# Graph convolution and mixture of experts: chunk maxima spread by TensorE, gate weights second in their queue, x in batches, gathers of edges first in theirs

## What is computed

```python
edge_index = jnp.stack([src, dst])
h = _layernorm(x)                                   # m, v over the 512 columns
agg = jax.ops.segment_sum(h[src], dst, num_segments=2500)
x = x + (jax.nn.relu((h + agg) @ gW1 + gb1) @ gW2 + gb2)

t = _layernorm(x)
gate = jax.nn.softmax(t @ Wg, axis=-1)              # [2500, 8]
topv, topi = jax.lax.top_k(gate, 2)
topv = topv / (jnp.sum(topv, axis=-1, keepdims=True) + 1e-06)
scores = jnp.zeros((2500, 8)).at[jnp.arange(2500)[:, None], topi].set(topv)
for e in range(8):
    ye = jax.nn.gelu(t @ eW1[e] + eb1[e], approximate=False) @ eW2[e] + eb2[e]
    x = x + ye * scores[:, e:e + 1]
```

## Time and profile before

| | |
|---|---|
| median of 3 runs | 671.99 us (671.09 to 674.37) |
| profiled execution: its own time | 672.53 us |
| profiled execution: its span | 670.8 us |
| TensorE busy | 564.6 us, 84% |
| VectorE | 408.1 us, 61% |
| ScalarE | 298.4 us, 44% |
| GpSimd | 251.4 us, 37% |
| first stage: TensorE's first product of the first layer, first of the sums | 29.80 us, 142.46 us |

### The profile page before, as it was taken

One profiled execution on the slowest core, in us unless ns is written; L12 is line 12 of the kernel. 1 busy time (PEld: TensorE's weight loads), 2 busy tenths in 40 slices (PEclk: granted clock), 3 DMA queues, 4 the chain that ended last, 5 costly groups with the idle time before them and its releaser, 6 DMA issues.

```text
span 670.8 us, 10239 instructions
## 1 busy us (share of the span) xinstructions
PE 564.6 (84%) x3667; PEld 438.6 (65%) x3668; DVE 408.1 (61%) x776; ACT 298.4 (44%) x569; POOL 251.4 (37%) x215
## 2 busy tenths in 40 slices
PE   0597979999999999999999999904999999999800
PEld 0486868766756666766666655804888888889800
DVE  3562566777468877976986131696656675454441
ACT  0265346533233224223322300528676776767662
POOL 5044112213007004200700411013577878787763
PEclk9999889999899999999999999956999999999955
DMA  9351400020001220311121121878589988899994
GB/s 241 89 139 47 140 1 1 1 74 1 1 11 53 78 63 2 93 47 48 47 79 60 48 80 59 267 259 246 129 171 193 185 194 181 180 204 199 179 172 63
DMA packets 41672, 72.50 MB, mean 108 GB/s; under 512 B 11315, under 2 KB 15547, under 8 KB 41106
## 3 DMA queue, kind: packets, MB, share of 16 engines
q0 software_dynamic: 12864, 29.74, 22.9%
q1 hardware_dynamic: 27394, 37.44, 18.7%
q10 hardware_dynamic: 1364, 4.66, 2.5%
HBM read 46.70 MB, written 26.17 MB: 109 GB/s over the span
## 4 chain that ended last, share of the span: by engine, by line
PE 58%; DMA 13%; POOL 9%; ACT 6%; issue 6%; DVE 5%; SPq 1%; ACTq 1%; POOLq 0%; DVEq 0%
PE psum L1291 25%; PE psum L1275 9%; PE psum L1211 8%; DMA out_x<-y,target_i 8%; PE psum L1328 6%; POOL out_x L581 6%; POOL xg L574 3%; DMA Wg_sb<-in_L_ffn_Wg 3%; PE psum L1433 2%; PE psum L1422 2%; PE psum L1200 1%; ACT y L781 1%; DMA slot_rows<-edge_pairs,start_i 1%; DMA w_raw<-in_L_ffn_W 1%; ACT h L658 1%
## 5 line engine op out<-in xcount | busy, mean ns | idle before, releaser
L962 DVE TENSOR_TENSOR hot_key<-iota_key,key_w 128x1200 f16<-128x1200 f16 x125 | 113.6, 909 | 67.8 <-PE psum L1275 66.5
L640 ACT ACTIVATE counts<-psum 128x400 bf16<-128x400 f32 x125 | 61.8, 506 | 155.9 <-PE psum L1275 155.6
L1291 PE MATMUL psum<-counts,z_hi 125*128 125x500 bf16 x400 | 102.2, 376 | 2.2 <-ACT h L658 1.6
L581 POOL DMA_INDIRECT out_x<-y,target_i x54 | 90.5, 1676 | 35.8 <-issue 12.5
L1291 PE MATMUL psum<-counts,z_lo 125*128 125x500 bf16 x400 | 101.2, 376 | 0.0
L1275 PE MATMUL psum<-hot_key,hot_lo 128*128 128x200 f16 x750 | 82.6, 250 | 7.3 <-ACT counts L640 7.3
L548 POOL TENSOR_TENSOR h_lo<-h,h_hi 128x500 fp32r<-128x500 f32 x16 | 23.5, 1500 | 169.5 <-ACT h_hi L665 169.5
L1275 PEld LDWEIGHTS psum<-hot_key,hot_lo 128*128 128x128 f16 x750 | 66.1, 98 | 28.5 <-ACT counts L640 8.4
L962 DVE TENSOR_TENSOR hot_lo<-iota_lo,lo_w 128x768 f16<-128x768 f16 x125 | 83.6, 669 | 0.0
L1211 PE MATMUL psum<-W_sb,xT 128*125 128x256 f32 (+1 forms) x320 | 77.3, 397 | 0.0
L574 POOL DMA_INDIRECT xg<-xt_d,token_i x56 | 58.0, 1036 | 38.8 <-DVE token_i L1118 22.1
(11 more groups left out here) (226 smaller groups left out, 1056.3 us busy)
## 6 DMA issues: line engine op xcount, KB each, us to landing
w_raw<-in_L_ffn_W SPq DMA_DIRECT2D x16, 512.0 KB, 6.8
b_now<-in_L_ffn_b SPq DMA_DIRECT2D x27, 256.0 KB, 4.6
x_res<-in_x SPq DMA_DIRECT2D x20, 224.0 KB
out_x<-x SPq DMA_DIRECT2D x20, 224.0 KB
xt_d<-xt SPq DMA_DIRECT2D x20, 224.0 KB
x_in<-in_x ACTq DMA_DIRECT2D x2, 1120.0 KB
x_in<-in_x SPq DMA_DIRECT2D x2, 1120.0 KB
W_sb<-in_L_gnn_W ACTq DMA_DIRECT2D x1, 1024.0 KB, 7.6
```

The source lines that it names most:

```text
L581: pool.indirect_dma_start(out=out[:, :], in_=y[:, k % 2, i], in_offset=None, out_offset=bass.IndirectOffsetOnAxis(ap=target_i[:, 2 * k + i ...
L640: act.activation(counts[:, it % 2, :, place:place + W], psum[:, WIN + w % 2, 0:MW].rearrange("p (w h) -> p h w", w=W), ACT.Copy).then_inc( ...
L962: ins = dve.tensor_tensor(hot[:, w % RING].rearrange("p s (n two) -> p s n two", two=2), iota[:].rearrange("p (o n two) -> p o n two", o=1 ...
L1291: ins = mm(psum[:, AGG + c, 0:GN], half[:, t, c * 128:(c + 1) * 128], counts[0:P, g % 2, t], start=(t == 0 and n == 0), stop=(t == T - 1 a ...
```

## The change

- TensorE spreads the chunk maxima: VectorE multiplies an identity matrix with the maxima (`hit[:, 1]`, 125 x 625), and TensorE multiplies that with ones, which puts all 625 maxima on each partition, in PSUM (`spans_spread`). `find_chunks` reads them there. The way through memory (`spans_d`, `spans_b`) stays for the general case alone. TensorE may not write these banks at tile 1 before `chunks_known`.
- SP's queue: gate weights between dst and src; edge pairs ahead of `dst_next`.
- x is loaded in the five batches of the statistics, each with its own semaphore (`load_rows`): three at the start, by ScalarE's queue, the fourth and fifth by SP at the old places.
- GpSimd makes `ones`, the identity and what the first steps need first, tables for the general case last, and issues both gathers ahead of all `low_parts`.
- VectorE: new order, below. TensorE: W1 turned ahead of the gate sum.
- Flaws and first row transposes after tile 5 (was 7), the flag after tile 7 (was 9), so windows start after tile 8. The last statistics follow `one_hots(9)` (was 5), their scales `one_hots(11)`.

```diff
-ROWS_AT, FLAG_AT, ROWS_FIRST = 7, 9, 4
+ROWS_AT, FLAG_AT, ROWS_FIRST = 5, 7, 4
...
-        def load_half(eng, n):
+        def load_rows(eng, b):
+            a, end = BATCHES[b]
+            place = a % (2 * HALF)
             for cut in CUTS:
-                eng.dma_start(x_in[cut, HALF * (n % 2):HALF * (n % 2 + 1)], x_tiles[cut, HALF * n:HALF * (n + 1)]).then_inc(x_in_sems[n], 16)
+                eng.dma_start(x_in[cut, place:place + end - a], x_tiles[cut, a:end]).then_inc(x_in_sems[b], 16)
...
                 sp.dma_start(dst_i[cut], dst.rearrange("(p e) -> p e", p=P)[cut]).then_inc(S["dst_in"], 16)
+            sp.dma_start(Wg_sb[:], Wg.rearrange("(k p) e -> p k e", p=128)).then_inc(S["wg_in"], 16)
             for cut in CUTS:
                 sp.dma_start(src_i[cut], src.rearrange("(p e) -> p e", p=P)[cut]).then_inc(S["src_in"], 16)
-            sp.dma_start(Wg_sb[:], Wg.rearrange("(k p) e -> p k e", p=128)).then_inc(S["wg_in"], 16)
-            sp.wait_ge(S["spans_ready"], 1)
-            sp.dma_start(spans_d.rearrange("a (p c) -> p a c", p=P), spans[:]).then_inc(S["spans_out"], 16)
             sp.wait_ge(S["tables"], 1)
             sp.dma_start(edge_pairs[E:E + SLOTS, :].rearrange("(o e) a -> o e a", o=1), pad_pairs[:]).then_inc(S["rows_out"], 16)
-            sp.wait_ge(S["spans_out"], 16)
-            sp.dma_start(spans_b[:], spans_d.rearrange("(o a) c -> o a c", o=1).broadcast_to([NW, 2, NCH])).then_inc(S["spans_in"], 16)
+            sp.wait_ge(S["keys_ready"], 1)
+            for cut in CUTS:
+                sp.dma_start(edge_pairs[0:E, :].rearrange("(p e) a -> p (e a)", p=P)[cut],
+                             pairs_sb[cut].rearrange("p e a -> p (e a)")).then_inc(S["rows_out"], 16)
             sp.wait_ge(S["next_blank"], 1)
...
-            sp.wait_ge(S["keys_ready"], 1)
-            for cut in CUTS:
-                sp.dma_start(edge_pairs[0:E, :].rearrange("(p e) a -> p (e a)", p=P)[cut],
-                             pairs_sb[cut].rearrange("p e a -> p (e a)")).then_inc(S["rows_out"], 16)
...
-            load_half(sp, 2)
+            load_rows(sp, 3)
...
+            pool.memset(ones[:], 1.0)
+            step(pool.memset(ident[:], 0.0))
+            pool.affine_select(out=ident[:], in_=ident[:], compare_op=ALU.not_equal, fill=1.0, base=0,
+                               pattern=[[-1, 128]], channel_multiplier=1).then_inc(S["ident_ready"], 1)
+            pool.memset(eps_t[:], EPS)
+            pool.iota(win_lo[:], pattern=[[HW, 2]], base=0, channel_multiplier=W, **small)
+            pool.memset(pad_pairs[:, :, 0], PAST)
+            pool.memset(pad_pairs[:, :, 1], -1.0).then_inc(S["tables"], 1)
...
-            def low_parts(a, b):
-
-                for t in range(a, b):
-                    pool.wait_ge(S["z_ready"], t + 1)
-                    pool.wait_ge(S["z_hi_ready"], t + 1)
-                    pool.tensor_tensor(z_lo[:, t], z[:, t % ZF], z_hi[:, t], ALU.subtract).then_inc(S["z_lo_ready"], 1)
-
-            low_parts(0, 2)
+                               pattern=[[1, W], [-1, T]], channel_multiplier=0).then_inc(S["tables"], 1)
             pool.wait_ge(S["chunks_known"], 1)
             for a in range(2):
                 pool.indirect_dma_start(out=bound_rows[:, a], out_offset=None, in_=dst.rearrange("(c e) -> c e", e=CH),
                                         in_offset=bass.IndirectOffsetOnAxis(ap=chunk_i[:, a:a + 1], axis=0),
                                         bounds_check=NCH - 1).then_inc(S["bounds_gathered"], 16)
-            low_parts(2, 4)
+            pool.iota(win_hi[:], pattern=[[HW, 2]], base=HW - 1, channel_multiplier=W, **small)
+            pool.iota(chunk_up[:], pattern=[[1, NCH]], base=1, channel_multiplier=0, **small)
+            pool.iota(chunk_down[:], pattern=[[-1, NCH]], base=NCH, channel_multiplier=0, **small)
+            pool.iota(gen_iota[:], pattern=[[1, MW]], base=0, channel_multiplier=0, **small).then_inc(S["tables"], 1)
             pool.wait_ge(S["starts_known"], 1)
             pool.wait_ge(S["rows_out"], 48)
             for a in range(2):
                 pool.indirect_dma_start(out=slot_rows[:, a].rearrange("w e a -> w (e a)"), out_offset=None, in_=edge_pairs[:, :],
                                         in_offset=bass.IndirectOffsetOnAxis(ap=start_i[:, a:a + 1], axis=0)).then_inc(S["gathered"], 16)
-            low_parts(4, T)
+
+            def low_parts(a, b):
+
+                for t in range(a, b):
+                    pool.wait_ge(S["z_ready"], t + 1)
+                    pool.wait_ge(S["z_hi_ready"], t + 1)
+                    pool.tensor_tensor(z_lo[:, t], z[:, t % ZF], z_hi[:, t], ALU.subtract).then_inc(S["z_lo_ready"], 1)
+
+            low_parts(0, T)
...
-            for n in range(2):
-                load_half(act, n)
-            act.wait_ge(S["tables"], 2)
+            for b in range(3):
+                load_rows(act, b)
+            act.wait_ge(S["tables"], 1)
...
-            dve.tensor_reduce(spans[:, 1], dst_v, AX.X, ALU.max).then_inc(S["spans_ready"], 1)
+            step(dve.tensor_reduce(spans[:, 1], dst_v, AX.X, ALU.max))
+            dve.wait_ge(S["ident_ready"], 1)
+            dve.tensor_tensor(hit[:, 1].rearrange("p (c q) -> p c q", c=CPP), ident[0:P, 0:P].rearrange("p (o q) -> p o q", o=1).broadcast_to([P, CPP, P]),
+                              spans[:, 1].rearrange("p (c o) -> p c o", o=1).broadcast_to([P, CPP, P]), ALU.mult).then_inc(S["spans_wide"], 1)
...
-                dve.wait_ge(S["spans_in"], 16)
+                dve.wait_ge(S["spans_spread"], 1)
+                largest = psum[0:NW, AGG + 2:AGG + 4].rearrange("p b n -> p (b n)")[:, 0:NCH]
                 for a in range(2):
-                    step(dve.tensor_scalar(hit[:, a], spans_b[:, 1], win_lo[:, a:a + 1], None, ALU.is_lt, ALU.add,
+                    step(dve.tensor_scalar(hit[:, 0], largest, win_lo[:, a:a + 1], None, ALU.is_lt, ALU.add,
                                            accum_out=first[:, a:a + 1]))
...
-            edge_sources()
+            find_chunks()
+            weight_scale()
             centre_gate()
-            weight_scale()
             statistics(0)
             scales(0)
             scale_weights()
+            edge_sources()
+            edge_keys()
             statistics(1)
             scales(1)
-            edge_keys()
+            find_starts()
             statistics(2)
             scales(2)
-            find_chunks()
             compare_edges()
+            close_rows()
             statistics(3)
-            scales(3)
-            find_starts()
-            close_rows()
...
+            scales(3)
...
-                if w == 5:
+                if w == 9:
                     statistics(4)
+                if w == 11:
                     scales(4)
...
-            pe.wait_ge(S["tables"], 2)
+            pe.wait_ge(S["spans_wide"], 1)
+            for b in range(2):
+                part = slice(512 * b, min(512 * (b + 1), NCH))
+                ins = mm(psum[0:NW, AGG + 2 + b, 0:part.stop - part.start], ones[0:P].broadcast_to([P, NW]), hit[:, 1, part], start=True, stop=True)
+            ins.then_inc(S["spans_spread"], 1)
+            pe.wait_ge(S["ident_ready"], 1)
+            pe.wait_ge(S["w1_most_ready"], 1)
+            for m in range(KC):
+                ins = pe.transpose(psum[:, WIN, m * 128:(m + 1) * 128], W1_most[:, m * 128:(m + 1) * 128], ident[:])
+            ins.then_inc(S["w1_turned"], 1)
             pe.wait_ge(S["wg_in"], 16)
             for k in range(KC):
                 ins = mm(psum[:, WIN + 1, 0:NE], ones[:].broadcast_to([128, 128]), Wg_sb[:, k], start=(k == 0), stop=(k == KC - 1))
             ins.then_inc(S["wg_summed"], 1)
-            pe.wait_ge(S["w1_most_ready"], 1)
-            for m in range(KC):
-                ins = pe.transpose(psum[:, WIN, m * 128:(m + 1) * 128], W1_most[:, m * 128:(m + 1) * 128], ident[:])
-            ins.then_inc(S["w1_turned"], 1)
...
+                if t == 1:
+                    pe.wait_ge(S["chunks_known"], 1)
```

52 lines of the change are left out of this document (22 added, 30 removed).

## The result

The changed kernel takes 662.16 us (median of 4 runs, 661.56 to 664.91); the kernel before took 671.54 us beside it. The ratio is 0.986, interval 0.982 to 0.990. On a second chip it was 0.982 (0.976 to 0.988). Both intervals lie wholly under 1. So 9.4 us went, where 19.25 were forecast, and the time lies above the range of 647 to 660. The profiled execution took 661.56 us, its span 659.8.

The account below looks back on a forecast made before the run. TensorE was taken to bound the first stage: a late start on the gate weights, then a chain of 20 tiles with waits. - 8.0 + 2.2 - 7.35 - 6.0 + 2.0 - 2.1 = - 19.25 us, so 652.5 us; range 647 to 660.

Parts of the forecast that it names:

- Step 1, the start: Before the first layer: VectorE's new order and earlier gate weights start it at about 21.8 instead of 29.80; minus 8.0 us.
- the start does not come sooner: Rival: gate weights land at 20.8 as ever, small pieces slow beside x; minus 1.6, not 8.0; 659 us; chance 0.10.
- Step 2, tiles 0 to 5: First tiles: VectorE's edge steps ahead of statistics make TensorE late by 1.3 and 0.9; plus 2.2 us (0 to 4).
- Step 3, the rows: Flaws and row transposes after tile 5: wait for gathered rows goes, minus 4.35; full clock behind it, minus 3.0 us.
- The clock was to stay: At the row transposes and their tile: full clock instead of half, 5.2 us instead of 8.25; minus 3.0 us.
- Step 4, windows: From tile 8, two windows a tile: minus 2.1, minus 6.0 for the 4.47 wait and slow return, plus 2.0 us.
- The three waits fewer: Three windows come after the last tile alone, so three waits of 0.70 us for ScalarE go; minus 2.1 us.
- The new wait: At tile 13's transposes TensorE waits while ScalarE stands at the root for batch 4's statistics; plus 2.0 us (1 to 3.5).
- The clock rival: New short waits at tiles 1, 2 and 12 lower the clock, 1.5 to 3.0 us each; 655.5 to 659; chance 0.14.
- more waits than I see: Rival: the new order of three engines has further waits, such as late bound gathers; 660 to 668 us; chance 0.07.
- Faster: The whole kernel takes measurably less time than before, 0.5% (3.4 us) being distinguishable; chance 0.96.

Follow-up runs that it names:

- before_wg_behind_w1: The kernel before with one edit, the gate weights behind W1 in ScalarE's queue: 668.37 us, ratio 0.991.
- The three repairs: Changed kernel with gate weights behind W1, fourth statistics behind the flag, last statistics behind window 7: 651.81 us, ratio 0.964 to the kernel before.

## Why the prediction was wrong

**Step 1, the start: the failed step.** Minus 8.0 was forecast, minus 3.28 came. VectorE's steps had the right sizes: search 12.82 to 14.92 as in the sum, from PSUM at 0.86 and 0.87 a pass, no dearer than from SBUF; product 0.81, the lower bound (16.6 + 4.96 is 21.6 and not 21.8, a slip of 0.2). What failed is the sentence that bounded the gate weights' landing by 15.08, "the time at which the transfer in this place (src) landed". A place in a queue is not a time. Src has 125 pieces of 2.5 KB; the gate weights have 512, and from 8 to 16 us each waits for one of ScalarE's. They landed at 19.4. Of the 3.28, 1.36 is their landing (19.44 for 20.80) and 1.92 is W1's transposes and the weight scale, which are done while they are awaited. The rival "the start does not come sooner" named the cause, small pieces beside x, and was given 0.10; it would have been right to ask how many pieces there are, a number that stood in the prediction. The Trainium skill (DMA: Bandwidth & Descriptors, "Queues, rings and completion order") speaks of a packet of several pieces at a time, by which the prediction had the gate weights in by 9 to 13, an estimate. Page and trace differ, and the measurement decides: here the packets that the trace counts alternate one for one, in stretches as short as 0.2 us, each of the small ones a single piece of 32 bytes. Cost: 4.7 us, shown by two edits. The step also gave the 8.0 to VectorE's new order; before_wg_behind_w1 starts as early with the old one, so it was the gate weights' landing that held the start in the kernel before.

**Step 2, tiles 0 to 5.** Plus 2.2 forecast. From the first layer's start to the flaws' sum it took 53.14 - 26.52 = 26.6; with the first tile at its 4.35 and five of 3.94, 24.05 would have been enough: plus 2.6. Right.

**Step 3, the rows.** Minus 7.35 forecast. The wait for the rows is gone, as forecast, but they landed at 46.7 and not at 37 to 44: the gathers went out at 33.50 (forecast 28.7) and took 13.2 us, where 8.5 was taken. With `dst_next` on 16 engines they took 9.9, so it was more than the text allowed for it. Missed was what VectorE has between the rows and the flag. The diff of the change has it, `statistics(3)`, but the step names no wait for its batch of x, whose landing it takes at the old 8 us from an issue at 35; it was issued at 39.4 and took 13.3; with the rows' transposes held by the flag, 2.67 of the gain is lost. The text weighed the four-engine rule for `dst_next` against the gathers alone. It is right, and its other victim is the batch of x queued behind on the same engines. The clock was to stay; it did in the profile of the result (61.84 - 56.40 = 5.44 us for the twelve transposes and the tile, forecast 5.2, so 2.8 gained of 3.0) and not in the second profile of the same kernel. That it stayed behind a wait of 3.07 is luck.

**Step 4, windows.** The three waits fewer are minus 2.6 (forecast 2.1). The new wait was foreseen with its place and its cause, ScalarE at the root for statistics behind window 9's one-hots, but as plus 2.0: it is 2.64, and 1.8 more for the tile behind it at the lower clock. The clock rival was listed beside the forecast as if it excluded the rest. Undersized by 2.4, shown by the run that moves the statistics.

**Sum.** 4.7 + 2.7 + 2.4, with 0.4 in step 2 and 0.2 in the row transposes, less 0.5 in the windows and 0.6 in a quicker first tile, is 9.3; forecast and result are 19.25 - 10.27 = 9.0 apart at the first sums, so 0.3 is not placed. The three repairs, one for each of the first three terms, bring the first sums to 119.5, where the forecast had 123.

**The rivals** were priced one at a time: start 659, clock 655.5 to 659. The first came in large part, the second at one of its three places (tile 13's transposes, called tile 12 there) for 1.8, and with them a third wait, VectorE's for the fourth batch of x, that none of them names. Together they lie outside a range that took in each alone. The measured 662.16 is inside "more waits than I see", 660 to 668, which had 0.07 and stood outside the range; its examples (bounds late, a slow search, a full ring) are not what came. That nothing behind the first sums changes was right to 0.7 us. "Faster" was right.

## What to carry to other kernels

Count a transfer's pieces, not its bytes: beside a queue of large rows each small piece waited for a row here, and a transfer of 16 KB landed when the other queue was empty. Put what is small and needed first into the queue of the large transfers, ahead of those that can wait (here behind W1 and ahead of x), or make it fewer pieces; in one line it was worth 5.4 us at the changed kernel's start and 5.7 us of the old kernel's time. Before crediting a new order with a gain, look for one landing that holds the old one. When a wait is moved away, look at what the waiting engine's list still has between the data and the signal, and give each new wait of 2.5 us or more the price of the slow clock as well.
